# Narrower causal-mask products and a values product that shares the bank ring, in an attention and gated feed-forward kernel

## The chip, the cores and the metric

The kernel runs on one core of one Trainium2 chip. The metric is the device time of one execution in microseconds (us). A core has TensorE (PE; its weight loads are listed apart as PEld), VectorE (DVE), ScalarE (ACT), GpSimd (POOL) and SyncE (SP), which here issues every transfer.

## The reference

For 16 sequences of 512 rows and 256 features: a layer norm, causal attention with 16 heads of 16 features, a gated feed-forward product, and their combination.

```python
xn = _layernorm(x, axis=-1)
# attention
scores = jnp.einsum('bhsd,bhtd->bhst', q, k)
mask = jnp.triu(jnp.ones((S, S), dtype=bool), k=1)
scores = jnp.where(mask, -jnp.inf, scores)
attn = jax.nn.softmax(scores / sqrt(D), axis=-1)
out = jnp.einsum('bhst,bhtd->bhsd', attn, v)
# feed forward
h = jax.nn.silu(gate) * up
g = _silu(_L0_ffn_ref(xn, ...))
x = x + s * g
```

## The kernel before

Work is cut into small units, each with a two-letter name, a batch offset and an index, and, where it uses PSUM, its banks. Every engine walks through the same list of units and does its own part of each (`step`, L697), so the list is the program order of all engines at once. The list of the first part is HEAD (L54), then PERIOD (L84) runs 13 times with the batch advancing by one, then TAIL (L98). In `sm 1 16 45` the unit is sm, for the batch one ahead, index 16, banks 4 and 5. Three batches are in work at a time: the scores and values of one, the feed-forward product of the same and the next, the projections of the one after.

The units that matter here:
- la, lm, lc, lt, lb, lx: the layer norm of a later batch. la takes statistics on DVE and a pow on POOL (L237); lb multiplies on POOL (L266, L268); lx writes the split input, xt_hi on ACT (L275) and xt_lo on DVE (L279). lx waits until all products that read the old xt are done, gu 5 the last of them (L273).
- qk, v, gg, gu, dn, op: products that use the whole TensorE array (`parts_product`, L191, line L194 in the trace), each value as a high and a low part. gg and gu are the gate and up products, hs splits their product (ACT, then POOL), dn is the down product, op the output product.
- sm: score products (L434) of a pair of heads on two halves of the array, 64 rows each, used only for the row maximum. mk adds the causal mask onto the same banks by two pairs of bfloat16 products (L447): the first pair covers the right 64 columns of the diagonal block, the second its 128 columns, both for up to four score matrices side by side. DVE then takes the maximum (L459). MAXIMA (L35) gives each of the 22 sm/mk of a batch its rows and the number of matrices: 4 for two of them, 2 for four, 1 for sixteen.
- mt: transposes the row maxima, whose negatives are copied by SP into a row of the query stack. zr clears that row again after the last st of a batch (L480).
- st: transposed score products (L496), 20 per batch; ACT takes the exponential into one of 5 slots (L504), POOL zeroes above the diagonal (L511).
- pv: values products (L529), 12 per batch, three parts for a group of four heads; parts 0, 1 and 2 accumulate into one bank. ACT copies it out (L535) after part 2. In this kernel the bank is a tensor of its own, PVB, outside the ring of 7; part 0 waits for the copy of the group ahead (L521).
- od, or, ob, on, os: the sums are read back, inverted (DVE), sent out, and read back as o_reciprocals by SP (ob); on multiplies on POOL (L570), os splits into o_hi (ACT, L577) and o_lo (DVE, L580), which op reads.

A unit that uses a ring bank first waits for what released the bank last (`prev`, L700): RELEASED (L42) names the semaphore of each kind. Ahead of the units, POOL fills the constants (L740 to L757): zeros, ones, the identity, the half identities and the mask, then v's ones and the row maxima. TensorE waits for the constants at L792.

```python
def prev(e, *also, banks=banks, beta=b + ahead):
    latest = {u[0]: u for u in sorted([users[n] for n in banks if n in users] + [(kind, beta, k) for kind, k in also])}
    for last, last_beta, last_k in latest.values():
        after(e, RELEASED[last], last_beta, last_k)
```

## Time and profile before

| What | us |
|---|---|
| median of 3 runs | 958.91 |
| lowest and highest run | 958.46, 959.35 |
| span of the profiled execution, first to last instruction | 956.8 |

The page gives no other time of the profiled execution than its span; the median of the runs is 2.1 us above it. Busy time per engine, from the same page:

| Engine | busy us | share |
|---|---|---|
| PE | 926.0 | 97% |
| PEld | 686.7 | 72% |
| DVE | 701.0 | 73% |
| ACT | 584.7 | 61% |
| POOL | 495.3 | 52% |

A row of the trace in order of time has its start, its duration, the engine, the line, the operation, what it writes and reads, its shape (partitions x elements, for products rows*columns of the weights, then the moving operand), and how many instructions were merged into it; in brackets the idle time before it and who ended that. Records of matmuls overlap, since they are pipelined, and their ends are modelled.

### The profile page before, as it was taken

To read this page: it belongs to the slowest core of one execution; us is meant where nothing else is said; L and a number is where in the kernel's file an instruction comes from. 1 tells how busy PE (TensorE), PEld (TensorE's weight loads), DVE (VectorE), ACT (ScalarE), POOL (GpSimd) and SP (SyncE) were. 2 spreads that over 40 slices of the span, in tenths; PEclk is the share of its full clock that TensorE was granted. 3 is DMA by queue.
4 is the path that set the end of the run, shared out by engine and by line. 5 is a ranking of instruction groups with operands and counts; after the bars stand their busy time and mean duration, and the time that the engine had idled before them with its cause. 6 is when DMAs were issued, how large, how long until landed. Compare 5 with 4: busy or idle time off the path is not lost.

```text
span 956.8 us, 22743 instructions
## 1 busy us (share of the span) xinstructions
PE 926.0 (97%) x9065; PEld 686.7 (72%) x9065; DVE 701.0 (73%) x950; ACT 584.7 (61%) x796; POOL 495.3 (52%) x672
## 2 busy tenths in 40 slices
PE   5999999999999999999999999999999999999994
PEld 4767767866868677686877768687686867768564
DVE  7976758687786877768687786867778686777823
ACT  6265665656576665757657575665657666575771
POOL 4252645646455473645547354473645647364553
PEclk9999999999999999999999999999999999999998
DMA  8613245343443534435353543534344353443323
GB/s 277 156 65 131 76 146 173 125 157 116 168 148 113 172 126 156 130 144 157 117 175 100 197 131 124 171 126 151 122 168 144 116 175 126 155 130 144 110 93 89
DMA packets 85467, 133.97 MB, mean 140 GB/s; under 512 B 13680, under 2 KB 35952, under 8 KB 85360
## 3 DMA queue, kind: packets, MB, share of 16 engines
q1 hardware_dynamic: 85360, 132.47, 41.4%
q8 instruction: 75, 1.23, 0.5%
q14 instruction: 32, 0.26, 0.1%
HBM read 53.22 MB, written 25.75 MB: 83 GB/s over the span
## 4 chain that ended last, share of the span: by engine, by line
PE 86%; issue 4%; ACT 3%; POOL 2%; DVE 2%; DMA 2%; SPq 0%; ACTq 0%; POOLq 0%; DVEq 0%
PE bank L194 45%; PE values L529 13%; PE bank L434 12%; PE bank L496 9%; PE bank L447 5%; POOL o_compact L570 2%; ACT probs L504 2%; DMA o_reciprocals<-scratch_r 1%; ACT o_hi L577 1%; DVE gated L379 1%; PE bank L465 1%; POOL probs L511 1%; DVE row_max L459 0%; PE bank L672 0%; DMA scratch_r<-sum_reciprocals 0%
## 5 line engine op out<-in xcount | busy, mean ns | idle before, releaser
L459 DVE TENSOR_REDUCE row_max<-bank 128x2 f32<-128x768 f32 (+3 forms) x352 | 384.9, 1124 | 69.1 <-PE bank L447 65.2
L504 ACT ACTIVATE probs<-bank 128x1024 f32<-128x1024 f32 x320 | 320.3, 1024 | 124.9 <-PE bank L496 123.2
L511 POOL TENSOR_SCALAR_AFFINE_SELECT probs<-probs 128x256 f32<-128x256 f32 (+1 forms) x448 | 195.5, 454 | 276.8 <-ACT probs L504 274.5
L529 PE MATMUL values<-probs,v 128*17 128x512 f32 (+3 forms) x2048 | 166.2, 436 | 3.1 <-POOL probs L511 3.0
L393 POOL TENSOR_TENSOR h_lo<-gated,h_hi 128x512 fp32r<-128x512 f32 x96 | 125.1, 1303 | 70.2 <-ACT h_hi L390 67.9
L434 PE MATMUL bank<-k_stack,q_stack 64*128 64x128 f32 (+3 forms) x1024 | 156.9, 366 | 2.5 <-DVE row_max L459 1.4
L496 PE MATMUL bank<-q_stack,k_stack 64*128 64x512 f32 (+3 forms) x1024 | 142.0, 350 | 1.2 <-DVE row_max L459 0.7
L434 PEld LDWEIGHTS bank<-k_stack,q_stack 64*128 64x128 f32 x1024 | 84.2, 185 | 69.5 <-issue 30.4
L496 PEld LDWEIGHTS bank<-q_stack,k_stack 64*128 64x128 f32 x1024 | 82.8, 186 | 39.2 <-issue 17.1
L366 DVE SCALAR_TENSOR_TENSOR gated<-gated,bank 128x512 f32<-128x512 f32 x96 | 65.9, 686 | 58.3 <-ACT gated L363 58.3
L194 PE MATMUL bank<-xt_hi,wg_hi 128*128 128x256 f32 x384 | 99.2, 292 | 2.3 <-DVE gated L379 2.3
L447 PE MATMUL bank<-causal_mask,half_identities_bf 64*128 64x128 bf16 (+3 forms) x1408 | 98.2, 226 | 0.6 <-issue 0.6
L194 PE MATMUL bank<-wd_hi,h_hi 128*128 128x256 f32 x384 | 93.5, 283 | 3.3 <-POOL h_lo L393 3.3
L194 PE MATMUL bank<-xt_hi,wu_hi 128*128 128x256 f32 x384 | 95.8, 286 | 0.2 <-issue 0.2
L194 PE MATMUL bank<-xt_lo,wg_hi 128*128 128x256 f32 x384 | 93.9, 279 | 0.0
L194 PE MATMUL bank<-xt_lo,wu_hi 128*128 128x256 f32 x384 | 93.1, 279 | 0.0
L194 PE MATMUL bank<-wd_hi,h_lo 128*128 128x256 f32 x384 | 92.8, 281 | 0.0
L308 ACT ACTIVATE qk_hi<-bank 128x512 fp32r<-128x512 f32 x64 | 38.4, 599 | 80.3 <-PE bank L194 70.9
L529 PEld LDWEIGHTS values<-probs,v 128*17 128x17 f32 x2048 | 44.8, 96 | 53.0 <-issue 44.1
L194 PEld LDWEIGHTS bank<-xt_hi,wg_hi 128*128 128x128 f32 x384 | 73.0, 190 | 7.9 <-DVE gated L379 2.7
L194 PEld LDWEIGHTS bank<-wd_hi,h_hi 128*128 128x128 f32 x384 | 73.2, 191 | 4.6 <-POOL h_lo L393 3.5
L194 PEld LDWEIGHTS bank<-xt_hi,wu_hi 128*128 128x128 f32 x384 | 72.2, 188 | 4.0 <-issue 1.7
(119 smaller groups left out, 1598.8 us busy)
## 6 DMA issues: line engine op xcount, KB each, us to landing
k_stack<-qk_hi SPq DMA_DIRECT2D x64, 256.0 KB, 2.5
q_stack<-qk_hi SPq DMA_DIRECT2D x64, 256.0 KB, 2.6
scratch_o<-o SPq DMA_DIRECT2D x64, 256.0 KB, 2.3
x_again<-x SPq DMA_DIRECT2D x16, 512.0 KB, 4.6
k_stack<-qk_lo SPq DMA_DIRECT2D x32, 256.0 KB, 2.5
q_stack<-qk_lo SPq DMA_DIRECT2D x32, 256.0 KB, 2.9
o_compact<-scratch_o SPq DMA_DIRECT2D x32, 256.0 KB
o_reciprocals<-scratch_r SPq DMA_DIRECT2D x32, 256.0 KB
```

Of the source, the lines that this page charges most:

```text
L194: last = nc.tensor.matmul(dst, r(lhs[a]), r(rhs[b]), start=start and j == 0, stop=stop and j == len(parts) - 1)
L308: signal(e.activation(r(QKP[0][:, k % 2, :]), PS[:, banks[0], :], ACT.Copy), "d_qh")
L366: signal(e.scalar_tensor_tensor(out=T[:, slot, :], in0=T[:, slot, :], scalar=1.0, in1=PS[:, banks[0], :], op0=ALU.add, op1=ALU.mult), "d_a")
L393: signal(e.tensor_tensor(r(HT[1][:, f:f + 2, :]).rearrange("p f s -> p (f s)"), T[:, slot, :], HT[0][:, f:f + 2, :].rearrange("p f s -> p ...
L434: nc.tensor.matmul(PS[:, n, j * keys:(j + 1) * keys], r(QS[par][low:low + STACK, pair, i * P:(i + 1) * P]), r(KS[par][low:low + STACK, pai ...
L447: last = nc.tensor.matmul(scores[:, :, i * P + 64 * upper:keys], IDB[low:low + 64, low + 64 - 64 * upper:low + 192 - 64 * upper], MASK[low ...
L459: signal(e.tensor_reduce(rows, scores, axis=AX.X, op=ALU.max), "d_sm")
L496: last = nc.tensor.matmul(PS[:, n, at:at + w], r(KS[par][low:low + STACK, pair, j * P:(j + 1) * P]), r(QS[par][low:low + STACK, pair, j * ...
L504: signal(e.activation(PR[:, (SCORES * beta + k) % SLOTS, :, :], both(banks), ACT.Exp, scale=SCALE_S), "d_ex")
L511: last = e.affine_select(out=diag, in_=diag, compare_op=ALU.is_ge, fill=0.0, base=0, pattern=[[0, many], [1, P]], channel_multiplier=-1)
L529: last = nc.tensor.matmul(PVB[32 * c:32 * c + VW, j * P:S], V[par][:, j, 4 * g + c, :], PR[:, (SCORES * beta + 5 * g + kind) % SLOTS, pari ...
L570: signal(e.tensor_tensor(OC[:], OC[:], RDEN[:], ALU.mult), "d_on")
```

## The change

The second pair of mask products covers 64 columns instead of 128. For that the mask is stored as 64 columns, and the weights (PICK) pick for each row of the diagonal block the mask row that holds for the left half or the right half; POOL builds both in more steps ahead of the units. The values product takes its bank from the ring, which grows from 7 to 8 banks; it is listed with a bank in all three tables and waits with `prev` in part 0. HEAD and TAIL keep their order, with bank 7 for pv except its first units of a period; PERIOD is a new order with new banks. The last op uses bank 7 for its second half. Of HEAD and TAIL only examples are shown.

```diff
--- before.py
+++ after.py
@@ -39,8 +39,8 @@
 PIECES = [[(0, 0, 0)], [(1, 0, 0)], [(0, 3, 384), (0, 1, 0)], [(1, 3, 384), (1, 1, 0)], [(0, 2, 0), (1, 2, 256)]]
 
 
-RELEASED = dict(gm="d_gm", tr="d_xl", qk="d_ql", v="d_v", gg="d_a", gu="d_h", dn="d_g", op="d_y", mt="d_nml", sm="d_sm", st="d_ex")
-RING = 7
+RELEASED = dict(gm="d_gm", tr="d_xl", qk="d_ql", v="d_v", gg="d_a", gu="d_h", dn="d_g", op="d_y", mt="d_nml", sm="d_sm", st="d_ex", pv="d_ov")
+RING = 8
 SLOTS = 5
 SCORES = 20
 
@@ -58,51 +58,51 @@
-    sm 0 14 56, st 0 1 01, lc 1 0, mk 0 14 56, st 0 2 34, st 0 3 56, sm 0 15 01, mk 0 15 01, st 0 4 34, pv 0 0, sm 0 16 01,
+    sm 0 14 56, st 0 1 01, lc 1 0, mk 0 14 56, st 0 2 34, st 0 3 56, sm 0 15 01, mk 0 15 01, st 0 4 34, pv 0 0 7, sm 0 16 01,
...
-    mk 2 12 01, gu 2 1 5, v 2 1 3, sm 2 13 01, mk 2 13 01, sm 2 14 45, hs 2 1, mk 2 14 45, gg 2 2 6, pv 1 9, sm 2 15 01,
-    mk 2 15 01, st 2 0 34, pv 1 10""")
+    mk 2 12 01, gu 2 1 5, v 2 1 3, sm 2 13 01, mk 2 13 01, sm 2 14 45, hs 2 1, mk 2 14 45, gg 2 2 6, pv 1 9 2, sm 2 15 01,
+    mk 2 15 01, st 2 0 34, pv 1 10 2""")
 
 PERIOD = table("""
-    ld 2 0, on 0 0, zr 0 0, ob 0 0, pv 0 11, sm 1 16 45, lt 2 0, st 1 1 01, la 2 0, st 1 2 23, mk 1 16 45, lm 2 0, gg 1 3 6,
-    os 0 0, lc 2 0, gu 1 2 1, gg 1 4 2, st 1 3 34, pv 1 0, st 1 4 56, sm 1 17 01, st 1 5 34, mk 1 17 01, od 0 1, gu 1 3 2,
-    sm 1 18 56, mk 1 18 56, hs 1 2, sm 1 19 01, st 1 6 34, mk 1 19 01, lb 2 0, pv 1 1, pv 1 2, sm 1 20 23, mk 1 20 23,
-    st 1 7 56, sm 1 21 01, mk 1 21 01, pv 1 3, st 1 8 23, or 0 1, st 1 9 45, ob 0 1, gg 1 5 6, lx 2 0, gu 1 4 0, gu 1 5 3,
-    dn 1 0 1, hs 1 3, mt 1 1 5, qk 2 0 2, on 0 1, hs 1 4, gg 2 0 0, qk 2 1 6, gu 2 0 5, hs 1 5, gg 2 1 1, qk 2 2 0, ls 2 0,
-    os 0 1, dn 1 1 6, gu 2 1 5, ls 2 1, st 1 10 12, st 1 11 34, pv 1 4, pv 1 5, sm 2 0 01, mk 2 0 01, ls 2 2, sm 2 1 56,
-    st 1 12 34, mk 2 1 56, op 0 0 2, sm 2 2 34, sm 2 3 01, mk 2 2 34, mk 2 3 01, qk 2 3 6, ls 2 3, op 0 1 2, hs 2 0,
-    sm 2 4 34, st 1 13 01, od 1 0, sm 2 5 56, mk 2 4 34, mk 2 5 56, v 2 0 2, sm 2 6 34, mk 2 6 34, st 1 14 01, sm 2 7 56,
-    mk 2 7 56, pv 1 6, sm 2 8 34, mk 2 8 34, st 1 15 12, xr 1 0, sm 2 9 56, mk 2 9 56, pv 1 7, st 1 16 34, sm 2 10 01,
-    mk 2 10 01, or 1 0, pv 1 8, sm 2 11 56, st 1 17 23, mk 2 11 56, mt 2 0 0, gg 2 2 1, sm 2 12 34, st 1 18 56, mk 2 12 34,
-    hs 2 1, v 2 1 2, st 1 19 01, sm 2 13 56, mk 2 13 56, pv 1 9, sm 2 14 23, mk 2 14 23, sm 2 15 01, st 2 0 56, mk 2 15 01,
-    pv 1 10""")
+    la 2 0, ld 2 0, ob 0 0, lt 2 0, pv 0 11 2, st 1 1 67, st 1 2 01, sm 1 16 34, mk 1 16 34, lm 2 0, gu 1 2 5, gg 1 3 2,
+    sm 1 17 67, lc 2 0, hs 1 2, sm 1 18 01, on 0 0, st 1 3 34, mk 1 17 67, mk 1 18 01, lb 2 0, os 0 0, gg 1 4 5, gg 1 5 2,
+    dn 1 0 3, gu 1 3 4, gu 1 4 6, od 0 1, gu 1 5 7, st 1 4 01, sm 1 19 23, or 0 1, sm 1 20 45, mk 1 19 23, lx 2 0, pv 1 0 6,
+    pv 1 1 6, pv 1 2 6, hs 1 3, mk 1 20 45, st 1 5 01, sm 1 21 23, mk 1 21 23, qk 2 0 7, hs 1 4, ob 0 1, qk 2 1 6, ls 2 0,
+    zr 0 0, hs 1 5, st 1 6 45, st 1 7 01, st 1 8 23, ls 2 1, gg 2 0 7, on 0 1, gg 2 1 6, mt 1 1 4, dn 1 1 5, os 0 1,
+    qk 2 2 0, sm 2 0 12, mk 2 0 12, st 1 9 67, sm 2 1 34, mk 2 1 34, pv 1 3 5, pv 1 4 5, pv 1 5 5, sm 2 2 67, st 1 10 01,
+    sm 2 3 23, mk 2 2 67, od 1 0, mk 2 3 23, gu 2 0 4, op 0 0 5, st 1 11 01, sm 2 4 67, st 1 12 23, mk 2 4 67, qk 2 3 4,
+    sm 2 5 01, ls 2 2, hs 2 0, st 1 13 56, sm 2 6 23, mk 2 5 01, ls 2 3, v 2 0 7, mk 2 6 23, sm 2 7 45, st 1 14 01, or 1 0,
+    pv 1 6 6, mk 2 7 45, sm 2 8 23, st 1 15 01, mk 2 8 23, op 0 1 7, sm 2 9 45, st 1 16 01, sm 2 10 23, mk 2 9 45,
+    mk 2 10 23, pv 1 7 6, pv 1 8 6, st 1 17 01, sm 2 11 45, mk 2 11 45, st 1 18 67, gu 2 1 2, mt 2 0 3, sm 2 12 01,
+    sm 2 13 45, st 1 19 67, mk 2 12 01, mk 2 13 45, gg 2 2 2, v 2 1 3, hs 2 1, sm 2 14 67, sm 2 15 01, mk 2 14 67, xr 1 0,
+    st 2 0 45, mk 2 15 01, pv 1 9 2, pv 1 10 2""")
 
 TAIL = table("""
...
-    hs 1 4, ob 1 1, gu 1 5 0, hs 1 5, zr 0 0, os 1 1, xr 1 0, zr 1 0, on 1 1, dn 1 1 6, op 1 0 1, op 1 1 4""")
+    hs 1 4, ob 1 1, gu 1 5 0, hs 1 5, zr 0 0, os 1 1, xr 1 0, zr 1 0, on 1 1, dn 1 1 6, op 1 0 1, op 1 1 47""")
@@ -147,12 +147,11 @@
         LOW1 = sb("low_parts_all", [1, 1])
         FLAG = sb("no_low_parts", [1, 1], INT32)
         IDF = sb("identity", [P, P])
-        IDB = sb("half_identities_bf16", [P, 2 * P], BF16)
-        MASK = sb("causal_mask", [P, 4, P + 64], BF16)
+        PICK = sb("mask_rows_bf16", [P, 2, P], BF16)
+        MASK = sb("causal_mask", [P, 4, 64], BF16)
         ZERO = sb("zeros", [P, 512], BF16)
 
         PS = ctx.enter_context(nc.psum_tensor("bank", [P, RING, 512], FP32))
-        PVB = ctx.enter_context(nc.psum_tensor("values", [P, 512], FP32))
 
         sems = {name: sem(name) for name in COUNT}
         s_flag, s_lowrow, s_half = sem("s_flag"), sem("s_lowrow"), sem("s_half")
@@ -335,7 +334,7 @@
             elif en == "act":
                 after(e, "f_v", beta, k)
                 if beta < 2:
-                    e.wait_ge(s_const, 9)
+                    e.wait_ge(s_const, 18)
                 signal(e.activation(V[par][:, 2 * k:2 * k + 2, :, 0:D].rearrange("p t h d -> p (t h) d"),
                                     PS[:, banks[0], :].rearrange("p (h d) -> p h d", d=D), ACT.Copy), "d_v")
 
@@ -440,19 +439,17 @@
             i, pairs = MAXIMA[k]
             keys, n, half = P * (i + 1), len(pairs), k // (len(MAXIMA) // 2)
             if en == "pe":
-                for upper in (1, 0):
+                for right in range(2):
                     for parity, m in enumerate(banks):
                         low = 64 * parity
                         scores = PS[:, m, 0:n * keys].rearrange("p (n t) -> p n t", n=n)
-                        last = nc.tensor.matmul(scores[:, :, i * P + 64 * upper:keys],
-                                                IDB[low:low + 64, low + 64 - 64 * upper:low + 192 - 64 * upper],
-                                                MASK[low:low + 64, 0:n, low:low + P - 64 * upper], start=False, stop=upper == 0,
-                                                skip_group_check=True)
+                        last = nc.tensor.matmul(scores[:, :, i * P + 64 * right:i * P + 64 * right + 64], PICK[low:low + 64, right, :],
+                                                MASK[low:low + 64, 0:n, :], start=False, stop=right == 1, skip_group_check=True)
                 signal(last, "f_sm")
             elif en == "dve":
                 after(e, "f_sm", beta, k)
                 if beta == 0:
-                    e.wait_ge(s_const, 10)
+                    e.wait_ge(s_const, 19)
                 at = pairs[0] % (PAIRS // 2)
                 rows = MX[:, half, 32 * half:32 * half + 32].rearrange("p (b n i) -> p b n i", b=2, i=TT)[:, :, at:at + n, i]
                 scores = both(banks)[:, :, 0:n * keys].rearrange("p b (n t) -> p b n t", n=n)
@@ -518,7 +515,7 @@
                 if k == 0:
                     after(e, "d_v", beta, 1)
                 if part == 0:
-                    after(e, "d_ov", beta, g - 1)
+                    prev(e)
                 after(e, "d_mk", beta, 5 * g + (1, 3, 4)[part])
                 for n in range((1, 2, 1)[part]):
                     for cp in range(2):
@@ -526,13 +523,13 @@
                         j, at = ((0, 0), ((1, 0), (3, 384))[n], (2, 256 * cp))[part]
                         for parity in range(2):
                             c = 2 * cp + parity
-                            last = nc.tensor.matmul(PVB[32 * c:32 * c + VW, j * P:S], V[par][:, j, 4 * g + c, :],
+                            last = nc.tensor.matmul(PS[32 * c:32 * c + VW, banks[0], j * P:S], V[par][:, j, 4 * g + c, :],
                                                     PR[:, (SCORES * beta + 5 * g + kind) % SLOTS, parity, at:at + S - j * P], start=part == 0, stop=part == 2)
                 signal(last, "f_pv")
             elif en == "act" and part == 2:
                 wait(e, s_ost, 16 * (4 * beta + g))
                 after(e, "f_pv", beta, k)
-                signal(e.activation(O[:], PVB[:], ACT.Copy), "d_ov")
+                signal(e.activation(O[:], PS[:, banks[0], :], ACT.Copy), "d_ov")
             elif en == "sp" and part == 2:
                 wait(e, s_oc[g // 2], 32 * beta)
                 after(e, "d_ov", beta, g)
@@ -583,7 +580,7 @@
             halves = beta == B - 1 and k == 1
 
             def product(j):
-                return PVB[:, 0:E] if halves and j == 1 else PS[:, banks[0], j * E:(j + 1) * E]
+                return PS[:, banks[1], 0:E] if halves and j == 1 else PS[:, banks[0], j * E:(j + 1) * E]
 
             if en == "pe":
                 after(e, "d_ol", beta, 1)
@@ -703,7 +700,7 @@
                         after(e, RELEASED[last], last_beta, last_k)
                 UNIT[kind](en, e, b + ahead, (b + ahead) % 2, k, banks, prev)
                 if kind in RELEASED:
-                    users.update((n, (kind, b + ahead, k)) for n in banks)
+                    users.update((n, (kind, b + ahead, k // 3 if kind == "pv" else k)) for n in banks)
 
 
         stage_p = PR[:].rearrange("p a b c -> p (a b c)")
@@ -742,15 +739,32 @@
             e.memset(ZERO[:], 0.0).then_inc(s_zeros, 1)
             e.memset(RDEN[:], 1.0).then_inc(s_ones, 1)
             e.memset(IDF[:], 0.0).then_inc(s_const, 1)
-            e.memset(IDB[:], 0.0).then_inc(s_const, 1)
+            e.memset(PICK[:], 0.0).then_inc(s_const, 1)
             e.memset(MASK[:], 0.0).then_inc(s_const, 1)
             e.memset(MINUS_HALF[:], -0.5).then_inc(s_const, 1)
             e.wait_ge(s_const, 4)
-            for m, first, n in ((IDF, 0, P), (IDB, 64, 2 * P)):
-                e.affine_select(out=m[:], in_=m[:], compare_op=ALU.not_equal, fill=1.0, base=first,
-                                pattern=[[-1, n]], channel_multiplier=1).then_inc(s_const, 1)
-            e.affine_select(out=MASK[:], in_=MASK[:], compare_op=ALU.is_ge, fill=MASKED, base=0,
-                            pattern=[[0, 4], [-1, P + 64]], channel_multiplier=1).then_inc(s_const, 1)
+            e.affine_select(out=IDF[:], in_=IDF[:], compare_op=ALU.not_equal, fill=1.0, base=0,
+                            pattern=[[-1, P]], channel_multiplier=1).then_inc(s_const, 1)
+            for low in (0, 64):
+                e.wait_ge(s_const, 5 + low // 64 * 3)
+                for side in range(2):
+                    rows = PICK[:, side, 64 * side:64 * side + 63]
+                    e.affine_select(out=rows, in_=rows, compare_op=ALU.not_equal, fill=1.0, base=-low,
+                                    pattern=[[-1, 63]], channel_multiplier=1).then_inc(s_const, 1)
+                all_masked = PICK[:, 1, 0:64]
+                e.affine_select(out=all_masked, in_=all_masked, compare_op=ALU.not_equal, fill=1.0, base=-low - 63,
+                                pattern=[[0, 64]], channel_multiplier=1).then_inc(s_const, 1)
+            e.affine_select(out=MASK[:], in_=MASK[:], compare_op=ALU.is_ge, fill=MASKED, base=-64,
+                            pattern=[[0, 4], [-1, 64]], channel_multiplier=1).then_inc(s_const, 1)
+            e.wait_ge(s_const, 12)
+            e.memset(MASK[0:64], 0.0).then_inc(s_const, 1)
+            e.wait_ge(s_const, 13)
+            e.affine_select(out=MASK[0:64], in_=MASK[0:64], compare_op=ALU.is_ge, fill=MASKED, base=0,
+                            pattern=[[0, 4], [-1, 64]], channel_multiplier=1).then_inc(s_const, 1)
+            for row in (63, 127):
+                e.wait_ge(s_const, 14 + row // 127)
+                e.affine_select(out=MASK[:], in_=MASK[:], compare_op=ALU.not_equal, fill=MASKED, base=-row,
+                                pattern=[[0, 4], [0, 64]], channel_multiplier=1).then_inc(s_const, 1)
             for v in V:
                 e.memset(v[:], 1.0).then_inc(s_const, 1)
             e.memset(MX[:], 0.0).then_inc(s_const, 1)
@@ -789,9 +803,9 @@
 
         @block.tensor
         def _(e):
-            e.wait_ge(s_const, 7)
+            e.wait_ge(s_const, 16)
             e.wait_ge(s_zeros, 1)
-            nc.tensor.matmul(PVB[:], ZERO[:, 0:P], ZERO[:], start=True, stop=True).then_inc(s_fixed, 1)
+            nc.tensor.matmul(PS[:, RING - 1, :], ZERO[:, 0:P], ZERO[:], start=True, stop=True).then_inc(s_fixed, 1)
             run("pe", e)
```

## Rows read from the trace of the kernel before

**Rows 1.** The page, part 4: the chain that ended last, share by engine.

```profile
PE 86%; issue 4%; ACT 3%; POOL 2%; DVE 2%; DMA 2%; SPq 0%; ACTq 0%; POOLq 0%; DVEq 0%
```

**Rows 2.** Stretches: length; busy us (instructions) of PE, PEld, DVE, ACT, POOL; clock, DMA.

```profile
23.00:40.00 17.00, 15.79 (x152) 12.58 (x152) 16.62 (x21) 4.26 (x7) 3.37 (x3) 1.00 0.82 217
...
516.17:573.43 57.26, 56.66 (x565) 42.16 (x563) 42.71 (x60) 35.76 (x50) 31.89 (x43) 1.00 0.42 142
```

**Rows 3.** TensorE in order of time, 532.3 to 550.3 us: start, duration, work.

```profile
532.58 0.28 PE L194 MATMUL bank<-xt_lo,wu_hi 128*128 128x256 f32 x1
532.79 0.73 PE L496 MATMUL bank<-q_stack,k_stack 64*128 64x512 f32 x4
533.45 1.49 PE L529 MATMUL values<-probs,v 128*17 128x384 f32 x24
534.87 0.66 PE L434 MATMUL bank<-k_stack,q_stack 64*128 64x128 f32 x8
...
547.71 0.26 PE L447 MATMUL bank<-causal_mask,half_identities_bf 64*128 64x64 bf16 x4
547.90 1.06 PE L529 MATMUL values<-probs,v 128*17 128x384 f32 x16
548.89 0.51 PE L496 MATMUL bank<-q_stack,k_stack 64*128 64x512 f32 x2
549.22 0.40 PE L434 MATMUL bank<-k_stack,q_stack 64*128 64x512 f32 x2
549.46 0.27 PE L447 MATMUL bank<-causal_mask,half_identities_bf 64*128 64x64 bf16 x4
549.66 0.63 PE L529 MATMUL values<-probs,v 128*17 128x256 f32 x8
```

**Rows 4.** TensorE in order of time, from a mask group into whole-array work.

```profile
538.63 0.42 PE L447 MATMUL bank<-causal_mask,half_identities_bf 64*128 64x128 bf16 x8
538.99 0.50 PE L194 MATMUL bank<-xt_hi,wq_hi 128*128 128x512 f32 x1
```

**Rows 5.** Groups by line and form, L447: busy us, mean ns, idle us before.

```profile
L447 PE MATMUL bank<-causal_mask,half_identities_bf 64*128 64x128 bf16 x640 | 68.4, 219 | 0.0
...
L447 PE MATMUL bank<-causal_mask,half_identities_bf 64*128 64x64 bf16 x512 | 49.8, 198 | 0.6 <-issue 0.6
...
L447 PE MATMUL bank<-causal_mask,half_identities_bf 64*128 64x256 bf16 x192 | 26.6, 272 | 0.0
...
L447 PE MATMUL bank<-causal_mask,half_identities_bf 64*128 64x512 bf16 x64 | 12.2, 376 | 0.0
```

**Rows 6.** In order of time, DVE and then PEld, 504 to 509.7 us.

```profile
507.45 0.69 DVE L580 TENSOR_TENSOR o_lo<-o_compact,o_hi 128x512 fp32r<-128x512 f32 x1 [0.71 <-ACT o_hi L577]
508.06 0.68 DVE L379 SCALAR_TENSOR_TENSOR gated<-bank,gated 128x512 f32<-128x512 f32 x1
...
508.80 0.19 PEld L434 LDWEIGHTS bank<-k_stack,q_stack 64*128 64x128 f32 x2 [0.30 <-DVE gated L379]
```

**Rows 7.** POOL in order of time, 0 to 30 us.

```profile
2.12 0.74 POOL L746 MEMSET causal_mask<- 128x768 bf16 x1
...
3.14 0.29 POOL L750 TENSOR_SCALAR_AFFINE_SELECT identity<-identity 128x128 f32<-128x128 f32 x1 [0.24 <-POOL minus_half L747]
3.39 0.40 POOL L750 TENSOR_SCALAR_AFFINE_SELECT half_identities_bf<-half_identities_bf 128x256 bf16<-128x256 bf16 x1
...
4.54 1.95 POOL L755 MEMSET v<- 128x1088 f32 x2
...
6.85 1.02 POOL L237 TENSOR_TENSOR mv<-var,minus_half 128x4 f32<-128x4 f32 x1
```

**Rows 8.** Groups by line and form, L504, L279 and L275.

```profile
L504 ACT ACTIVATE probs<-bank 128x1024 f32<-128x1024 f32 x320 | 320.3, 1024 | 124.9 <-PE bank L496 123.2 <-PE values L529 1.1
...
L279 DVE TENSOR_TENSOR xt_lo<-x_transposed,xt_hi 128x1024 fp32r<-128x1024 f32 x15 | 19.1, 1270 | 16.9 <-ACT xt_hi L275 16.9
...
L275 ACT ACTIVATE xt_hi<-x_transposed 128x1024 fp32r<-128x1024 f32 x15 | 15.9, 1061 | 11.9 <-PE bank L194 9.8 <-POOL x_transposed L268 2.0
```

38 lines of the change are left out of this document (19 added, 19 removed).

## The prediction, made before the changed kernel was run

> **What bounds the kernel now.** I read the busy times first, in the table above: TensorE is busy 97% of the span. The chain that ended last says the same with lines: 86% of it is TensorE, "issue" 4%, everything else 10% [rows 1]. Then stretches of time, because the kernel is one start, thirteen equal periods and one end: the period from 516.17 to 573.43 has TensorE busy 56.66 of 57.26 us and VectorE busy 42.71; in the start, from 23 to 40 us, VectorE is busy 16.62 of 17.00 and TensorE 15.79 [rows 2]. So a period is as long as TensorE's own work plus its few gaps, and only the start has another bound.
>
> What that work consists of shows in the order of time. Matmuls overlap in their records, so I compare ends (start plus duration) of neighbouring rows: the distance is what a unit adds. Three kinds of product alternate: 64-row pairs (sm, mk, st), whole-array products (qk, v, gg, gu, dn, op, mt) and values products (pv). Changing kind costs extra [rows 3]. Entering the 64-row kind from the whole array: two st products of 512 columns end at 533.52, 0.66 after 532.86; inside the kind one such pair takes 0.22 (549.62 less 549.40), so 0.66 - 0.44 = 0.22. Entering it from values: 549.40 less 548.96 is 0.44, so 0.22. Entering values: the last part (pv of part 2) takes 550.29 less 549.73 = 0.56; inside a values run it takes 1.42 (534.94 less 533.52) less 0.99 (548.96 less 547.97) = 0.43, so 0.13. Entering the whole array: the first product of qk, 512 columns, ends at 539.49, 0.44 after the mask group's 539.05 [rows 4]; as above 0.22 of that are the columns, so 0.22. All this passes for "busy".
>
> **The narrower mask product.** Each mk keeps four products, but the second pair has 64 columns per score matrix in place of 128. Mean durations by form: 64 columns 0.198, 128 columns 0.219, 256 columns 0.272, 512 columns 0.376 us [rows 5]. The step from 256 to 128 is 0.053, from 512 to 256 it is 0.104, from 128 to 64 it is 0.021 by the means and 0.027 by halving 0.053; I take 0.024. It is not saved everywhere. Eight 128-column sm products, four pairs, add 0.59 after a values run (535.53 less 534.94 [rows 3]); less the 0.22 of entry that is some 0.09 a pair, nearly twice their columns (0.053 each by the steps above). I read it as the pace of float32 weight loads. So where a 64-row float32 product follows a mask product of 128 columns (0.053), the load, begun with the mask product, is late either way, and shortening gives nothing. In the new table, of 16 mk with one matrix 12 are followed by whole-array, values or mk work and 4 by sm or st: 12 x 0.024 = 0.29. The four with two matrices are followed by pv, mk, mk and gg: 4 x 0.053 = 0.21. The two with four: 2 x 0.10 = 0.20. Sum 0.70 a period, 9.1 in thirteen. Outside the periods, 38 of the 60 mk of the head lie behind 60 us, where TensorE is the bound, and 6 in the tail: 44/22 x 0.70 = 1.4. Ends: 0.5 a period if the 0.024 is nothing, 0.85 if every one is saved.
>
> Against this stands a rule. Four mask products with their four weight loads end 0.11 us after the product ahead of them (549.73 less 549.62 [rows 3]). The Trainium skill (TensorE: Matmul & The Clock Gate, section "LDWEIGHTS (loading the stationary operand)") gives a load P/1.2 ns, 107 for the 128 columns here, whatever the moving operand has; by it the mask pairs would be held by loads and 10.5 us of my sum would be gone. The row disagrees for these bfloat16 operands, while the float32 pairs above agree with it.
>
> **The new order.** The old table has 9 runs of pv and 8 of whole-array work in a period, each entered and left: 9 x (0.13 + 0.22) + 8 x (0.22 + 0.22) = 6.67. The new one has 5 and 10: 1.75 + 4.40 = 6.15. That is 0.52; I take 0.45, since each price is read to 0.02 only and runs that begin or end with mt may differ: 5.9 in thirteen. Three times in the new table mk itself comes first after pv or v, which the trace does not show; that entry costs between nothing and 0.22, and I take 0.22, as the nearest rows do. At nothing it would be 3 x 0.22 x 13 = 8.6 less.
>
> **Waits inside a period.** One has a name: sm 1 17 starts its load 0.30 late, on its bank's last reader, the multiply at 508.06; that stands in VectorE's queue behind o_lo of os 0 0 at 507.45, which idled 0.71 for ACT [rows 6]. os 0 0 hangs on the read back of the reciprocals (ob 0 0), which SP issues behind zr 0 0, and that waits for st 1 19. The new table moves zr 0 0 far back, starts ob 0 0 early, and gives sm 1 17 banks 6 and 7, last read by ACT for st 1 1. On SP, what zr 0 0 is moved past (ob, lt, lm, lc, od, ls) comes sooner; who waits for zr is sm 2 0, and between them stand two gg, a dn and a qk, 46 products of at least 0.11, 5 us for one small transfer, which covers it. On POOL, on 0 0 goes from first to behind hs 1 2; lb (two long multiplies) now has the six-unit whole-array run as cover. Since pv shares the ring, its first part waits for a bank like others; banks 2, 5 and 6 were given up several units earlier each time, so I cost it at nothing; uncovered it would wait for one ScalarE or VectorE read, 0.6 to 1.2. New waits I cannot exclude. I take the 0.30 as gone and 0.05 back: 0.25 x 13 = 3.3. Ends: 0.7 a period gained (every gap) and 0.5 lost.
>
> **The start.** The mask is now built by POOL in more steps, and POOL lies on the chain there: the multiply ahead (pow for the first layer norm, L237) starts at 6.85, directly behind POOL's memsets [rows 7]. Before, from the mask's memset at 2.12 to v's memset at 4.54 it is 2.42. Now: mask memset of 256 elements 0.25 (a third of 0.74), minus_half 0.10, wait on the engine's own result 0.24 (the idle ahead of 3.14), identity 0.29, wait 0.24; three selects of 64 columns 0.6 (identity starts 0.25 ahead of the next, 128 columns less is some 0.05 cheaper); wait 0.24; three more 0.6; select of 256 elements 0.40; then four steps (memset 0.3, selects 0.4, 0.4, 0.4), each behind a wait of 0.24: 2.46. Sum 5.42, 3.0 more. VectorE's x_in, the transposes and everything behind wait for pow; from 23 to 40 us VectorE is full, so little of it is made up. I take +2.9; ends 1.0 (weight transfers would have been late anyway) and 3.3.
>
> **Sum.** -9.1 - 1.4 - 5.9 - 3.3 + 2.9 = -16.8. Against the profiled execution's span, 956.8, that gives 940.0; the median of the runs, 958.9, stands 2.1 above this span, and less 16.8 it is 942.1. The transfers are the same in number and size; op's last half moves from the old values bank to bank 7, the same memory.
>
> **Rivals.** (a) The gaps of the period vanish whole and the mk entries after pv are cheap: another 0.4 a period, 5 us, 937. For it: bank reuse distances in the new table are mostly longer. Chance 0.20. (b) The longer runs of sm and st crowd VectorE and ScalarE, gaps grow by 0.6 a period, 8 us: 950. For it: VectorE would be busy 42.7 of 55.5; against it: the whole-array runs between leave it time. Chance 0.12. (c) The mask products gain nothing, because their weight loads, whose number and size stay, set their pace and not their columns: 942.1 + 9.1 + 1.4 = 952.6. For it: the float32 pairs behave so; against it: the steps between the forms and the 0.11. Chance 0.06. The Trainium skill's rule on loads, cited above, is this case. (d) Slower: qk 2 0 waits for xt. The copy xt_hi must wait for gu 1 5, since it overwrites its operand; it now follows the exp of st 1 4 on ACT. From gu's end: st 0.43 and exp 1.02, the copy 1.06, xt_lo 1.27 [rows 8], the row maximum of mk 1 19 beside them, some 0.1 of hand-over: 3.9. TensorE's work to qk is st, two sm, mk, three pv, mk, st, sm, mk: 0.43 + 0.47 + 0.08 + 2.3 + 0.29 + 0.28 + 0.24 + 0.08 = 4.2. Slack 0.3; old, dn and mt (2.9) covered a chain of 2.5. A wait decides from 16.8/13 = 1.3 us a period; with 1.6 (an exp and a row maximum more ahead of the copy) it is 942.1 + 20.8 = 962.9. Chance 0.06.
>
> **How the numbers follow.** Forecast 0.56. The range 933 to 951 holds it, (a) and (b), and leaves (c) and (d) and a little of the others outside; at the low end every gap and the cheap entries are gained, at the high end 0.7 a period is missed. Slower by over 0.2%, about 1.9 us, what a measurement can tell: (d) less a part, 0.05; within 0.2%: 0.01; faster: 0.94.
>
> **What would show it.** Right: periods of some 55.5 us (57.26 in the one quoted); L447 with 1024 products of 64 columns, 256 of 128 and 128 of 256, none of 512; no gap ahead of sm 1 17; pow at about 9.8 us. Wrong: TensorE idle in periods on xt_lo, row_max or probs; periods above 56.9; or mask groups of one matrix still adding 0.10.

## The result, and the profile after

The changed kernel takes 987.66 us (median of 4 runs, 981.24 to 990.08) where the kernel before takes 959.13 on the same chip: a ratio of 1.0283, 95% interval 1.026 to 1.0306. It is slower by 28.5 us; forecast was 942.1, with 933 to 951 as the range. The profile's page:

```profile
span 988.4 us, 22707 instructions
...
PE 920.5 (93%) x9065; PEld 692.4 (70%) x9065; DVE 695.1 (70%) x950; ACT 582.6 (59%) x796; POOL 491.9 (50%) x681
...
PE 47%; DMA 20%; SPq 9%; POOL 9%; DVE 8%; ACT 3%; issue 3%; POOLq 0%; DVEq 0%; ACTq 0%
```

TensorE is busy 5.5 us less than before (926.0), and the span is 31.6 longer, so TensorE now waits. In the chain that ended last it has 47% where it had 86% [rows 1]; transfers and their issues (DMA and SPq) have 29%. To see where, I took the thirteen periods of both kernels in one stretch each. Of the kernel before, then of the one after (windows; the first number is the length, then busy us of PE, PEld, DVE, ACT, POOL, the granted clock, DMA share, GB/s):

```profile
161.90:900.60 738.70, 735.67 (x7305) 547.63 (x7305) 554.54 (x752) 464.55 (x637) 398.08 (x534) 1.00 0.42 143
```

```profile
166.20:931.00 764.80, 729.57 (x7306) 551.85 (x7304) 548.55 (x754) 462.40 (x638) 392.99 (x533) 0.98 0.42 137
...
607.00:611.50 4.50, 4.50 (x44) 1.70 (x44) 2.03 (x2) 1.16 (x2) 0.63 (x1) 0.62 0.02 4
...
605.74:613.74 8.00, 8.00 (x85) 4.92 (x86) 3.88 (x4) 2.65 (x3) 1.04 (x2) 0.79 0.10 36
547.67:555.67 8.00, 8.00 (x100) 5.97 (x100) 5.57 (x6) 2.76 (x4) 1.04 (x2) 1.00 0.10 36
```

The periods grew by 26.1 us: TensorE's busy time fell by 6.1 and its idle time rose from 3.0 to 35.2. The start grew by 4.3 (161.90 to 166.20). For what it waits, the waits of the kernel after (us in all, times, longest):

```profile
DVE stats L224 <- DMA x_in<-x: 25.3, 14, 3.7
...
PE bank L433 <- DMA q_stack<-qk_hi: 22.2, 13, 2.4
...
PE bank L493 <- DVE row_max L456: 7.2, 9, 2.2
...
PE bank L193 <- DVE xt_lo L278: 4.4, 11, 0.5
```

The largest wait of TensorE comes 13 times, once a period: sm 2 0 (L433) waits for q_stack. On SP and on TensorE, in order of time, one such place of the kernel after:

```profile
598.69 0.61 SPq L480 DMA_DIRECT2D q_stack<-zeros  x1
599.35 0.54 SPq L321 DMA_DIRECT2D q_stack<-qk_hi  x1
599.93 2.23 SPq L321 DMA_DIRECT2D q_stack<-qk_lo  x1
602.20 0.94 SPq L321 DMA_DIRECT2D q_stack<-qk_hi  x1
```

```profile
547.67 0.66 PE L433 MATMUL bank<-k_stack,q_stack 64*128 64x128 f32 x8 [2.27 <-DMA q_stack<-qk_hi]
...
591.82 0.63 PE L526 MATMUL bank<-probs,v 128*17 128x256 f32 x8 [0.79 <-POOL probs L508]
592.38 0.23 PE L446 MATMUL bank<-causal_mask,mask_rows_bf 64*128 64x64 bf16 x4
...
592.76 0.40 PE L433 MATMUL bank<-k_stack,q_stack 64*128 64x512 f32 x2
593.00 0.23 PE L446 MATMUL bank<-causal_mask,mask_rows_bf 64*128 64x64 bf16 x4
...
605.74 0.66 PE L433 MATMUL bank<-k_stack,q_stack 64*128 64x128 f32 x8 [1.60 <-DMA q_stack<-qk_hi]
...
607.17 4.04 PE L526 MATMUL bank<-probs,v 128*17 128x512 f32 x32
```

Between the transfers of ls 2 0 and ls 2 1 stands the zeros' transfer of zr 0 0. The second issue behind it, q_stack<-qk_lo, takes 2.23 us in place of 0.61. TensorE stands still 1.60 us. Its granted clock is still 1.00 from 605.74 to 607.00 and 0.62 over the 4.5 us after that (the window above), partly at 1.2 GHz in place of 2.4: 32 values products take 4.04 us. But a gap does not always do this. Behind the longer one of 2.27 us at 547.67 the clock stays at 1.00 over 8 us, in which 100 products start; behind the one at 605.74 it is 0.79 over 8 us, with 85. Of the fifteen gaps of 1.3 us and more in the thirteen periods, seven were followed by the lower clock. The chain that ended last holds this piece, and another one ahead of it:

```profile
571.39 0.41 SPq L215
...
571.85 4.93 DMA x_in<-x
...
578.92 1.03 POOL mv L236
...
579.97 2.74 DMA scratch_m<-mv
...
582.73 3.36 DMA mean_and_rstd<-scratch_m
...
586.22 2.47 POOL x_transposed L265
...
588.75 2.43 POOL x_transposed L267
...
602.20 3.45 DMA q_stack<-qk_hi
```

That is the layer norm of the batch two ahead, from the load of x to xt_lo. It ends just ahead of qk 2 0 (the 4.4 us on xt_lo). Of the kernel before, on SP and on VectorE:

```profile
497.54 0.41 SPq L211 DMA_DIRECT2D x_in<-x  x1
```

```profile
502.68 1.40 DVE L225 BATCH_NORM_STATS2 stats<-x_in 128x6 f32<-128x256 f32 x4
```

There too the load was issued right behind the transfers of the row maxima, and the statistics began 5.1 us after it, but VectorE did not wait: the load had landed (3.6 us from issue to landing, the median of the fifteen). Now the large x_again (L215) is issued ahead of the load, the load takes 5.5 us to land, and VectorE, which has la first in its list, is free 1.3 us before it lands.

The mask products did what they should: in the rows of TensorE above, a group of one matrix ends at 593.23, 0.07 after the scores ahead of it (593.16), where it was 0.11 [rows 3]; behind values products it ends at 592.61, 0.16 after them (592.45). Their forms (count, busy us, mean ns), to set beside [rows 5]:

```profile
L446 PE MATMUL bank<-causal_mask,mask_rows_bf 64*128 64x64 bf16 x1024 | 53.8, 194 | 0.6 <-issue 0.6
L446 PE MATMUL bank<-causal_mask,mask_rows_bf 64*128 64x128 bf16 x256 | 16.6, 222 | 0.0
L446 PE MATMUL bank<-causal_mask,mask_rows_bf 64*128 64x256 bf16 x128 | 13.3, 279 | 0.0
```

Last, the start, on POOL and on VectorE, to set beside [rows 7]:

```profile
6.95 1.94 POOL L769 MEMSET v<- 128x1088 f32 x2
...
9.12 1.03 POOL L236 TENSOR_TENSOR mv<-var,minus_half 128x4 f32<-128x4 f32 x1
10.10 1.47 POOL L646 CAST probs<-probs 128x1536 f32<-128x1536 int32 x1
```

```profile
10.18 3.65 DVE L258 TENSOR_SCALAR x_in<-x_in,mv 128x256 f32<-128x256 f32 x4 [4.57 <-POOL mv L236]
```

The pow starts at 9.12 where it was 6.85: 2.27 later, where 3.0 was worked out.

### The profile page after: what moved, and what is told of

It is laid out like the page before. It is cut to its first block, busy times and chain, and to the rows that moved or that the text cites. A ratio compares the mean times of both kernels' runs of the same rounds, so it can differ in the third digit from the quotient of the medians.

```text
span 988.4 us, 22707 instructions
## 1 busy us (share of the span) xinstructions
PE 920.5 (93%) x9065; PEld 692.4 (70%) x9065; DVE 695.1 (70%) x950; ACT 582.6 (59%) x796; POOL 491.9 (50%) x681
## 4 chain that ended last, share of the span: by engine, by line
PE 47%; DMA 20%; SPq 9%; POOL 9%; DVE 8%; ACT 3%; issue 3%; POOLq 0%; DVEq 0%; ACTq 0%
PE bank L193 22%; PE bank L526 9%; DMA x_in<-x 7%; PE bank L433 7%; SPq L321 6%; PE bank L493 6%; DMA q_stack<-qk_hi 5%; DMA mean_and_rstd<-scratch_m 4%; POOL x_transposed L265 3%; POOL x_transposed L267 3%; PE bank L446 3%; DMA scratch_m<-mv 2%; DVE xt_lo L278 2%; SPq L474 2%; DVE stats L224 1%
## 5 line engine op out<-in xcount | busy, mean ns | idle before, releaser
L508 POOL TENSOR_SCALAR_AFFINE_SELECT probs<-probs 128x256 f32<-128x256 f32 (+1 forms) x448 | 190.8, 441 | 248.2 <-ACT probs L501 245.6
L526 PE MATMUL bank<-probs,v 128*17 128x512 f32 (+3 forms) x2048 | 166.1, 455 | 2.9 <-POOL probs L508 2.8
L433 PE MATMUL bank<-k_stack,q_stack 64*128 64x128 f32 (+3 forms) x1024 | 144.8, 349 | 23.9 <-DMA q_stack<-qk_hi 22.2
L433 PEld LDWEIGHTS bank<-k_stack,q_stack 64*128 64x128 f32 x1024 | 82.5, 187 | 58.6 <-issue 36.1
L493 PEld LDWEIGHTS bank<-q_stack,k_stack 64*128 64x128 f32 x1024 | 85.4, 186 | 41.6 <-issue 20.3
L526 PEld LDWEIGHTS bank<-probs,v 128*17 128x17 f32 x2048 | 51.2, 100 | 74.7 <-issue 63.2
L193 PE MATMUL bank<-xt_hi,wu_hi 128*128 128x256 f32 x384 | 98.7, 294 | 0.4 <-issue 0.4
L365 DVE SCALAR_TENSOR_TENSOR gated<-gated,bank 128x512 f32<-128x512 f32 x96 | 63.2, 681 | 49.5 <-ACT gated L362 49.5
L446 PE MATMUL bank<-causal_mask,mask_rows_bf 64*128 64x64 bf16 (+2 forms) x1408 | 81.0, 207 | 0.6 <-issue 0.6
L446 PEld LDWEIGHTS bank<-causal_mask,mask_rows_bf 64*128 64x128 bf16 x1408 | 39.7, 95 | 53.6 <-issue 45.5
```

The lines of the kernel that those rows point to most:

```text
L193: last = nc.tensor.matmul(dst, r(lhs[a]), r(rhs[b]), start=start and j == 0, stop=stop and j == len(parts) - 1)
L365: signal(e.scalar_tensor_tensor(out=T[:, slot, :], in0=T[:, slot, :], scalar=1.0, in1=PS[:, banks[0], :], op0=ALU.add, op1=ALU.mult), "d_a")
L433: nc.tensor.matmul(PS[:, n, j * keys:(j + 1) * keys], r(QS[par][low:low + STACK, pair, i * P:(i + 1) * P]), r(KS[par][low:low + STACK, pai ...
L446: last = nc.tensor.matmul(scores[:, :, i * P + 64 * right:i * P + 64 * right + 64], PICK[low:low + 64, right, :], MASK[low:low + 64, 0:n, ...
L493: last = nc.tensor.matmul(PS[:, n, at:at + w], r(KS[par][low:low + STACK, pair, j * P:(j + 1) * P]), r(QS[par][low:low + STACK, pair, j * ...
L508: last = e.affine_select(out=diag, in_=diag, compare_op=ALU.is_ge, fill=0.0, base=0, pattern=[[0, many], [1, P]], channel_multiplier=-1)
```

## The experiments

The theories, after this reading: (Z) the place of zr 0 0 makes the second issue behind it slow; (L) the layer norm's chain, from the load of x on, is late; (S) POOL's longer constants cost the start; and as rival (O) the new order itself crowds the engines, whatever the transfers do. Ratios are to the kernel before, on the same chip; a period is the mean distance of the thirteen in the profile (56.8 before, 58.8 after). Where a kernel has more lines than the one after, its line numbers are higher.

### The old order with the new mask and ring (e1_old_order)

```diff
 PERIOD = table("""
-    la 2 0, ld 2 0, ob 0 0, lt 2 0, pv 0 11 2, st 1 1 67, ...
+    ld 2 0, on 0 0, zr 0 0, ob 0 0, pv 0 11 7, sm 1 16 45, ...
```

The PERIOD table of before, with bank 7 for every pv.

> The changed kernel with PERIOD put back to the order and banks of before (pv on bank 7 throughout): only the narrower mask products, pv in the ring and the longer building of the mask are left of the change. Theory 1, the new order ties each period to a chain of transfers (x_in, statistics, scratch_m, mean_and_rstd, the POOL multiplies, xt, qk, the stacks, sm 2 0) that is longer than TensorE's work in it: the slowdown is gone, 959.1 less about 10.7 for the mask products and more about 4.5 for the start (the transposes began at 13.9 us in place of 9.3), so about 953. Rival 2, VectorE and ScalarE are crowded by longer runs of sm and st: also about 953. Rival 3, the mask products or the ring wait of pv themselves cost time: above 970.

Measured: 955.28 us, ratio 0.9953 (0.9939 to 0.9967), period 56.4. So the loss comes with the new order, and mask and ring alone gain. Windows of this kernel:

```profile
165.00:898.00 733.00, 727.97 (x7308) 545.95 (x7308) 555.57 (x752) 464.60 (x638) 397.91 (x533) 1.00 0.43 144
```

Busy time fell by 7.7 us from 735.67; idle time rose by 2.0 (it stands ahead of pv 1 0 and sm 1 17, which the faster TensorE reaches sooner, as I read it). The first period starts 3.1 us later than before.

### Load and statistics a period earlier (e2_early_stats)

```diff
-    la 2 0, ld 2 0, ob 0 0, lt 2 0, ... mk 1 16 34, lm 2 0, gu 1 2 5,
+    ob 0 0, lt 2 0, ... mk 1 16 34, gu 1 2 5,
-    qk 2 3 4, ... st 1 17 01, sm 2 11 45,
+    qk 2 3 4, ld 3 0, ... st 1 17 01, la 3 0, lm 3 0, sm 2 11 45,
```

HEAD has the same for batch 3, and lm's first transfer waits until the rows of the batch ahead have been read.

> The changed kernel with its new order, but ld, la and lm of the next batch issued earlier, in the period before (ld behind qk 2 3, la and lm behind st 1 17; the head does the same for its last batch), so that VectorE no longer waits for x_in and the chain is shorter by the load, the statistics and one transfer, some 7 to 10 us. Theory 1: TensorE's waits on q_stack, xt_lo and row_max (22, 4 and 7 us in all) mostly vanish, periods fall from 58.9 to about 55.6, the time to 945 to 950. Rival 2: periods stay above 58, since VectorE and ScalarE do the same work at the same places; time above 980.

Measured: 995.66 us, ratio 1.0373 (1.0356 to 1.0391): slower still, though the statistics no longer waited for x; 945 to 950 was expected. The surprise is on VectorE and POOL, in order of time:

```profile
587.06 2.92 DVE L578 TENSOR_TENSOR o_lo<-o_compact,o_hi 128x512 fp32r<-128x512 f32 x1 [1.18 <-ACT o_hi L575]
```

```profile
586.99 2.45 POOL L266 TENSOR_TENSOR x_transposed<-x_transposed,mean_and_rstd 128x1024 f32<-128x1024 f32 x1
```

POOL's multiplies, no longer held by the late rows, now lie beside o_lo, which takes 2.92 us for its 0.69 [rows 6], in twelve of the thirteen periods.

### The statistics' rows not transferred (e3_no_rows)

```diff
-            if en == "sp":
+            if en == "sp" and beta < 2:
...
-                wait(e, s_bc, 16 * beta)
+                wait(e, s_bc, 16 * min(beta, 1))
```

It leaves out the two transfers of mean and rstd from batch 2 on; POOL multiplies by the rows of batch 1.

> The changed kernel with part of the computation left out: from batch 2 on, the transfer of mean and reciprocal deviation out to memory and back (lm, lc) is not made, and the POOL multiplies use the rows of batch 1. The chain loses two transfers (about 6 us a period); VectorE still waits for x_in, and the order is the new one. Theory 1: the wait for q_stack and xt_lo goes, the wait of the row maximum behind x_in may stay; periods of 55.6 to 56.5 us, time 945 to 958. Rival 2: periods stay above 58, time above 980.

Measured: 990.74 us, ratio 1.0307 (1.0286 to 1.0328). The chain was cut and nothing was won: the multiplies again lay beside o_lo (2.92 us). By itself this run does not clear theory L; together with e2 it shows that moving the multiplies has a price of its own, which theory L had not.

### The old order with late constants (e4_late_const)

```diff
+        def late_constants(e):    # PICK, MASK, v's ones, row maxima
...
+                if k == 3:
+                    late_constants(e)
```

On top of e1: only identity and minus_half come first, the rest is built behind the weight casts.

> The kernel of the first run of this set (old order, new mask) with the building of mask, mask rows, v's ones and the row maxima moved on POOL from ahead of the first pow to behind the two casts of the weights. If the start term is this POOL work alone, the pow starts at 5.5 to 6.8 us in place of 9.1 and the time falls by 4 to 5.5 us, to about 948; if the start is bound by the weights' transfers or by VectorE, it falls by less than 2.

Measured: 951.44 us, ratio 0.9911 (0.9894 to 0.9927); the first period starts at 160.9 against 165.0, and the period stays 56.4. So S is real and worth about 4 us. Its rows on VectorE:

```profile
7.50 1.38 DVE L285 TENSOR_SCALAR x_in<-x_in,mv 128x256 f32<-128x256 f32 x4 [1.14 <-POOL mv L263]
```

The four x_in take 1.38 here, 2.53 in e1 and 3.65 in the kernel after, where POOL's casts run beside them (from 10.10 and 11.79, some 1.5 us each).

### One unit moved: the zeros early (e5_zero_row_early)

```diff
-    sm 1 17 67, lc 2 0, hs 1 2,
+    sm 1 17 67, lc 2 0, zr 0 0, hs 1 2,
...
-    zr 0 0, hs 1 5, st 1 6 45,
+    hs 1 5, st 1 6 45,
```

> The changed kernel with one unit moved: zr 0 0 (the transfer that clears a row of the query stack) from between ls 2 0 and ls 2 1 to behind lc 2 0, early in the period. In every period of the changed kernel the transfer q_stack<-qk_lo, sixth in an unbroken row of three k_stack transfers, the zeros and q_hi, took SP 2.1 us to issue in place of 0.6, and sm 2 0 then waited 1.7 us. Theory 4, the zero row in that place is what makes sm 2 0 late: the issue goes back to 0.6, the wait on q_stack and the dips of the granted clock behind it vanish, 1.8 us and 0.7 us a period, time 955 to 963. Rival 5, qk 2 1 and sm 2 0 simply stand too close and any six transfers are held: only the 0.6 of the zero row's own issue is gained, time 975 to 983.

Measured: 953.85 us, ratio 0.9947 (0.9931 to 0.9964): one unit of one queue takes back 3.4% of the time, more than the whole loss. The issues of q_stack<-qk_lo in the periods (count: min/median/max ns), after and then here. Half of the 26 are those of ls 2 1, which stood behind the zeros:

```profile
L321 SPq DMA_DIRECT2D q_stack<-qk_lo x26: 603/1467/2251, 188.0 to 914.4; - x26
```

```profile
L321 SPq DMA_DIRECT2D q_stack<-qk_lo x26: 607/617/871, 185.5 to 883.1; - x26
```

TensorE's wait on q_stack is gone. Behind the zeros' new place the second issue starts 2.1 us or more later, and none takes over 0.82. The windows and the products in time say what else went:

```profile
164.30:899.40 735.10, 719.12 (x7308) 548.10 (x7306) 547.65 (x753) 462.66 (x638) 393.00 (x534) 1.00 0.44 143
```

```profile
588.13 2.35 PE L526 MATMUL bank<-probs,v 128*17 128x512 f32 x32
```

Of the 29.7 us that the periods lost, 19.3 were TensorE's idle time (35.2 to 16.0) and 10.4 its busy time (729.57 to 719.12), at a granted clock of 1.00 for 0.98: the same 32 products take 2.35 for 4.04. What stays of idle time is, for the larger part, st 1 3 (7.8 us), behind row_max, and qk 2 0 (4.1), behind xt_lo, with VectorE still waiting 26.1 us for x.

### Zeros early, statistics early, and the multiplies behind o_lo (e6, e7, e8)

```diff
                 wait(e, s_bc, 16 * beta)
+                if beta > 2:
+                    after(e, "d_ol", beta - 2, 0)
```

With this wait lb's multiplies start behind o_lo. e6 is e5 with it and e2's early statistics, e7 is e2 with it (zeros late, as in the kernel after), e8 is e6 with late constants.

> The second run's kernel (early load and statistics) with the zero row moved as in the first run of this set, and with the POOL multiplies of lb waiting for o_lo of os 0 0. In the second and third run, in which the rows were there earlier, o_lo on VectorE took 2.92 us in place of 0.69 in every period, beside the two POOL multiplies. If chain, zero row and that collision are all that holds the new order, periods come down to 55.0 to 55.6 us (TensorE's own work, 54.9), time 940 to 950. If VectorE or ScalarE are simply crowded (rival 2), periods stay above 57, time above 965.

> The second run's kernel (early load and statistics) with only the wait of lb for o_lo added, the zero row where the change has it. If the collision of o_lo with the POOL multiplies is what ate the gain of the early statistics, o_lo is back at 0.69 us and the time falls from 995.7 to 968 to 980, with the q_stack wait of 1.7 us a period still there. If not, it stays above 990.

> The second kernel of this set with the constants built late on POOL as well: 4 us less than that one (the e4 step took 3.8), so 936 to 946.

Measured: e6 958.49, ratio 0.9994 (0.9982 to 1.0006); e7 979.25, 1.0203 (1.0182 to 1.0225); e8 951.88, 0.993 (0.9914 to 0.9947). Tile o_lo in e7 (min/median/max ns):

```profile
L580 DVE TENSOR_TENSOR o_lo<-o_compact,o_hi x32: 683/688/1462, 121.7 to 969.3; 128x512 fp32r<-128x512 f32 x32
```

e7 against e2 differs by that wait alone: 16 us less, and o_lo is back at 0.69. Against e6, e7 has the late zeros and pays 20.8 us for them: Z again, in another setting. e6 against e5 was a miss: x comes in time, but la, put among the last sm and mk, now holds the row maxima, and sm 2 11 and sm 2 13 wait for banks (from their start to the next unit's 0.97 and 0.86 us for 0.39 and 0.24 in e5). e8 missed its 936 to 946 too, though the late constants gave 6.6 us over e6.

### The statistics beside dn, and the copy first (e9, e10)

```diff
-    qk 2 0 7, hs 1 4, ob 0 1, qk 2 1 6, ... mt 1 1 4, dn 1 1 5, os 0 1,
+    qk 2 0 7, hs 1 4, ob 0 1, ld 3 0, qk 2 1 6, ... mt 1 1 4, la 3 0, dn 1 1 5, lm 3 0, os 0 1,
```

e9 is e8 with ld, la and lm there. e10 is e9 with lx 2 0 moved from behind mk 1 19 to ahead of st 1 4.

> As e8_all, but the early load behind qk 2 0 and the early statistics ahead of dn 1 1, in the long whole-array run, instead of among the last sm and mk, where sm 2 11 and sm 2 13 waited some 1.3 us a period for row_max. If those waits came from the place of the statistics on VectorE, they vanish and periods fall from 56.3 to 55.2, time 937 to 943. If VectorE is crowded there anyway (rival 2), it stays at 950 to 953.

> The third kernel of this set with lx 2 0 ahead of st 1 4, so that ScalarE copies xt_hi before it takes the exp of st 1 4. In e8_all qk 2 0 took 1.84 us in place of 1.60, waiting for xt_lo. If the exp ahead of the copy is what makes it late, 0.2 us a period go, 2 to 4 us in all; if the exp moved behind is then waited for by pv or st 1 5, nothing is gained.

Measured: e9 947.24, ratio 0.9856 (0.984 to 0.9872), period 55.9; e10 975.22, 1.0153 (1.0136 to 1.017), period 58.0. e9 is 0.7% faster than e8 by the ratios, less than expected (937 to 943); it shows that part of what e6 and e8 lost belonged to that place of la. From e10 2 to 4 us were hoped for, and it is 28 us slower. e10 shows rival (d)'s trade from the other side; waits:

```profile
PE bank L558 <- POOL probs L540: 26.6, 15, 2.2
```

With the copy ahead of the exp of st 1 4, qk 2 0 no longer waits, but pv 1 2 does, 2 us each period. Neither of the two places tried is free. The granted clock of the thirteen periods is 1.00 here, though TensorE stands still for 1.8 to 2.2 us in each; one of these gaps alone was followed by the lower clock.

### The kernel before with only zr moved (e11_before_zero_late)

```diff
-    ld 2 0, on 0 0, zr 0 0, ob 0 0, pv 0 11,
+    ld 2 0, on 0 0, ob 0 0, pv 0 11,
...
-    gu 2 1 5, ls 2 1,
+    gu 2 1 5, zr 0 0, ls 2 1,
```

> The kernel before, with zr 0 0 alone moved to where the change has it, between ls 2 0 and ls 2 1. If the zeros' transfer in that place is what holds the next issues, q_stack<-qk_lo takes SP some 2.1 us here too, in every period (median 0.604 before). Its price should be small here: the old order has dn, gu, two st and two pv, some 6 us, between qk 2 2 and sm 2 0, and the stack had landed 3 us ahead; ob 0 0 is no longer behind zr 0 0, which may give back the 0.3 a period of sm 1 17. Time 953 to 962. If issues stay at 0.6, the place alone is not the cause and it is the pairing with the shorter distance.

Measured: 952.40 us, ratio 0.9911 (0.9895 to 0.9928): faster. SP in order of time:

```profile
524.40 0.63 SPq L483 DMA_DIRECT2D q_stack<-zeros  x1
525.07 0.54 SPq L322 DMA_DIRECT2D q_stack<-qk_hi  x1
525.65 2.20 SPq L322 DMA_DIRECT2D q_stack<-qk_lo  x1
```

The slow issue is there (2.20). In eleven of the thirteen periods the second issue takes 2.10 to 2.22; in the other two the delay is shared by the first (1.27 and 1.52) and the second (1.49 and 1.22). It costs nothing, since in the old order sm 2 0 comes late enough behind qk. So Z needs two things: the held issue and an order without slack behind it. And the freed ob 0 0 pays: windows of this kernel,

```profile
162.60:895.50 732.90, 732.90 (x7308) 547.90 (x7308) 554.86 (x753) 465.44 (x638) 393.13 (x533) 1.00 0.44 144
```

no idle time is left of 3.0 us.

### Both mends, then the load too (e12, e14)

e12 is the kernel after with e5's zeros and e4's late constants. e14 adds the load alone (not the statistics) a period earlier, and lb's wait for o_lo:

```diff
-    la 2 0, ld 2 0, ob 0 0,
+    la 2 0, ob 0 0,
...
-    mk 2 4 67, qk 2 3 4,
+    mk 2 4 67, qk 2 3 4, ld 3 0,
```

> The changed kernel with the zero row early (953.9 alone) and the constants built late on POOL (3.8 gained in the old order): the two terms add, 949 to 951.

> The two-moves kernel of the new order (zero row early, constants late: 956.8) with ld alone a part of a period earlier, behind qk 2 3 instead of behind mt 2 0 and the large x_again transfer, and lb waiting for o_lo; the statistics stay at the period's start. There VectorE waited for x_in, and st 1 3 behind it for row_max, 0.3 to 3 us a period. If the late load is what is left of the new order's loss, periods fall from 56.7 to 55.4 to 55.8 and the time to 940 to 945. If not the load but the length of the chain behind it is, it stays above 950.

Measured: e12 956.79, ratio 0.9959 (0.9945 to 0.9973); e14 946.20, 0.9868 (0.9846 to 0.9889). e12 was a miss: the constants gave 2.8 us at the first period, and the periods took them back (56.8 for 56.5). There st 1 3 waits up to 3.0 us behind x. Waits of e14:

```profile
DVE stats L251 <- DMA x_in<-x: 2.2, 2, 1.2
```

With the load early this falls from 27.4 us (e12) to 2.2, the wait of st 1 3 is gone, and the ratio falls by 0.9%. It takes 5.2 us to land even so; it is issued earlier. lb's wait for o_lo had nothing to mend in e12, where o_lo takes 0.69 in every period, and it keeps it so here. That is theory L, and the load is the part of it that matters. The time is just above the 940 to 945 that was expected. Windows of e14:

```profile
161.30:886.50 725.20, 714.57 (x7308) 548.19 (x7306) 550.24 (x754) 462.77 (x638) 394.44 (x534) 1.00 0.45 145
```

### The fastest: the old order, the new mask (e13_old_order_best)

e4 with zr 0 0 behind lc 2 0, which frees ob 0 0 as in e11:

```diff
-    ld 2 0, on 0 0, zr 0 0, ob 0 0, pv 0 11 7, ... os 0 0, lc 2 0, gu 1 2 1,
+    ld 2 0, on 0 0, ob 0 0, pv 0 11 7, ... os 0 0, lc 2 0, zr 0 0, gu 1 2 1,
```

> The old order with the new mask products and the constants built late (951.4 before), and zr 0 0 moved behind lc 2 0, so that neither ob 0 0 nor the stacks' transfers stand behind it. The move alone gave 8 us in the kernel before (960.6 to 952.4), by ob 0 0. If that gain and the mask's are separate, this is 943 to 945 and faster than every other kernel here; if the mask had already taken up those gaps, 948 to 951.

Measured: 942.29 us (941.59 to 942.62), ratio 0.9824 (0.9807 to 0.984), faster than both kernels. Windows:

```profile
161.60:884.90 723.30, 723.16 (x7306) 545.47 (x7306) 555.71 (x754) 465.49 (x637) 393.30 (x534) 1.00 0.43 146
```

TensorE is idle for 0.14 us in thirteen periods, and its busy time is 9.7 below e11's. The time is that of the forecast (942.1) by luck, since the order is the old one. And the held issue is here too, behind the zeros in their early place, on another tensor's transfer:

```profile
556.90 0.58 SPq L509 DMA_DIRECT2D q_stack<-zeros  x1
557.58 0.61 SPq L575 DMA_DIRECT2D sums<-scratch_o  x1
558.23 2.09 SPq L576 DMA_DIRECT2D o_compact<-scratch_o  x1
```

In nine of the thirteen periods it takes 1.79 to 2.27 us, in two 1.16 and 1.48, in two 0.60, and TensorE waits for none of it. The new order's e14 has less to do (714.57) but 10.6 of idle time.

## Why the prediction was wrong

Point by point, by its own steps:

**Waits inside a period: the step that failed.** It said of the moved zr: "who waits for zr is sm 2 0, and between them stand two gg, a dn and a qk, 46 products of at least 0.11, 5 us for one small transfer, which covers it." The cover was counted for the zeros' own transfer and not for those queued behind it. In the place it goes to, SP stands in the middle of the six stack transfers of ls 2 0 and ls 2 1, on which the same sm 2 0 waits; the zeros add 0.65 of issue and hold a later issue 1.6 longer, 2.3 us in a chain that ends only when the last q_stack has landed. For all new waits 0.05 was taken; this one is 2.3 a period (58.8 less 56.5 in e5), idle time and clock together. Of the 29.7 us in thirteen periods the lower clock can account for the 10.4 of busy time: behind seven gaps, six of them waits for q_stack, it was 0.79 over 8 us, and seven times 0.21 x 8 is 11.8 us, an estimate. The other half of the step held: with ob 0 0 freed, the 0.30 ahead of sm 1 17 went, in e11 with all other idle time (3.0 us; 3.3 taken).

**The same step, what it did not look at.** The slack of ld 2 0 was used up as well, and the sum had nothing for it: la first on VectorE, x_again ahead of the load on SP, 5.5 us to land for 3.6. No run parts these three. VectorE's 25.3 us on x, st 1 3 behind it, and part of qk 2 0's wait follow; e14, with the load earlier, takes VectorE's wait and that of st 1 3 away and leaves 2.8 of the 4.4 us on xt_lo. By the profiles it is 1.0 us a period (e12's 56.8 less e14's 55.8), by the ratios 0.7 (0.9% over thirteen periods).

**The narrower mask product: right.** 9.1 us in thirteen periods were worked out. e13 against e11, busy time of TensorE: 9.7 less (723.16 from 732.90; e13 also has the ring of 8 and the late constants, which have no product in a period). e1 against before gives 7.7, where gaps stand in both and can hide a part. The forms show 194 ns for 64 columns and 222 for 128. Rival (c), loads setting the pace, is refuted: a group of one matrix adds 0.07 us now for 0.11, with its loads unchanged. The rule cited there (the Trainium skill, TensorE: Matmul & The Clock Gate, section "LDWEIGHTS (loading the stationary operand)") has four loads at 107 ns each; with two side by side, as an estimate from it, that is 0.21. The trace has a third of it for these bfloat16 weights, and the measurement decides. The prediction had passed over the section behind it on that page, "Weight-path perf modes — Fast Weight Load (FWL) and DoubleRow", which has weights of 128 columns that are not float32 loaded faster; the trace agrees in kind, with some 95 ns for each of these loads and 190 for those of float32.

**The new order's work: right in kind.** Busy time of the thirteen periods is 16.6 below before in e5 and 21.1 in e14, against 9.1 + 5.9 = 15.0 worked out. The excess is 1.6 and 6.1. Part of it is the entry of mk behind values, taken at 0.22 with nothing as the lower end: by the rows at 592.38 it is some 0.09 (0.16 less the group's own 0.07), and for three a period that is an estimate of 5.1 us in thirteen. But idle time ahead of a unit also hides its entry, so these differences are not the order's alone. The gain is never reached: 16.0 and 10.6 us of idle time stand beside it.

**The start: right in kind, mis-sized.** 2.9 was taken. e4's constants give 4.1 back, with the pow at 6.44 for 6.85 before, so 3.7 is the cost in e1. The pow itself is late by 2.27, less than the 3.0 of the sum; the rest is x_in, 2.53 and 3.65 us for 1.38 beside POOL's cast, which the sum did not have.

**The rivals.** (d) named the right kind of thing, a chain into the next batch that ends just behind its reader, and priced it at 1.6 us a period with a chance of 0.06. It was there (qk 2 0 on xt_lo, 4.4 us in all), but not the one that decided; it looked along ACT and VectorE, and the chain that decided runs through SP. (b), crowding, was not what made the kernel after slow: e9 and e14 keep the order, but for the units moved, and are faster than before. Crowding appeared only where I put la badly (e6, e8). Of (a), the cheap entry of mk came true (0.09 for 0.22); that all gaps go did so in the old order (e11, e13) and not in the new one.

**Left open.** Why the second issue behind the zeros is held, and mostly not the first: the transfer differs from its neighbours in that it goes to 4 partitions, but no run tried another shape of it. Why the clock fell behind some gaps and not behind others as long. Why e5's and e4's gains do not add in e12, while e8 over e6 has the constants' gain whole (6.6 us): e14 shows that e12's loss goes with the late load, not how. And whether the new order can be freed of its last 10.6 us of idle time; 7.3 us of e14's idle time in all stand ahead of sm units, and the trace names no releaser for them.

## What to carry to other kernels

When a transfer moves in a queue, follow the transfers behind it, not only the one that moved: take each one's issue time from the trace, and the chain to the unit that waits for the last to land. An order that removes changes of kind can also remove slack, so every hand-over across an engine or a queue needs its slack worked out anew, loads of the next batch included. A gap in TensorE can be paid twice, by its length and by the clock after it; look at the clock behind each gap before you count that.

## What the runs showed of the hardware

- **An issue on SP can be held.** q_stack<-qk_lo takes 0.60 us to issue in most places. As the second behind the zeros' transfer it takes 2.09 to 2.25 in every period of the kernel after and 2.10 to 2.22 in eleven of thirteen in e11; with the zeros moved away it is 0.62 (e5). It is not that transfer's own: in e13 o_compact<-scratch_o stands second behind the zeros and takes 1.79 to 2.27 in nine of thirteen periods.
- **A short gap can lower the clock, and often does not.** After 1.60 us of idle time at 605.74 the granted clock was 1.00 for 1.26 us and then 0.62 over 4.5 us, between its levels of 1.2 and 2.4 GHz. Ahead of the gap TensorE had been busy with whole-array products. After 2.27 us of idle time in the same place of another period (547.67) it stayed at 1.00. The kernel after has the lower clock behind seven of fifteen such gaps, e10 behind one of thirteen of 1.8 to 2.2 us.
- **VectorE and POOL hold each other up.** o_lo, with two inputs in SBUF, takes 0.69 us alone and 2.92 when it starts beside a POOL multiply of 2.45 (e2); the wait that parts them is worth 16 us (e7). The Trainium skill (SBUF — State Buffer, section "Who interferes with whom") says that a DVE instruction with two SBUF inputs contends with a GpSimd instruction that reads SBUF; the trace agrees, and here the one that started 0.07 later took 2.23 us longer, nearly the whole of the other's 2.45. The four x_in, with one tensor input, went from 1.38 to 3.65 beside two POOL casts of some 1.5; the same section allows that for tensor_scalar in its 2-port modes, and no run here shows which mode they had.
- **A bfloat16 mask group is cheaper than its loads suggest.** Four loads and four products of 64 columns add 0.07 us to the products around them.
